# Inverse norms by plain tensor-tensor operations and the feed-forward affine step on ScalarE, in a Mamba and local-attention kernel

## The reference

```python
for i in range(6):
    x = attn_layer(shift_tokens(x), Wqkv[i], q_scale[i], k_scale[i], Wo[i]) + x
    x = ffn_layer(shift_tokens(x), ln_g[i], ln_b[i], W1[i], b1[i], W2[i], b2[i]) + x

def attn_layer(x, Wqkv, qs, ksc, Wo):      # 16 heads of 64, windows of 32 tokens
    q, k, v = jnp.split(x @ Wqkv, 3, -1)
    ...
    q = l2norm(q) * qs                     # t / max(norm(t), 1e-12), per head
    k = l2norm(k) * ksc
    q = q * cos * scale + rotate_half(q) * sin * scale
    k = k * cos / scale + rotate_half(k) * sin / scale
    return local_attention(q, k, v) @ Wo   # softmax over this and the last window

def ffn_layer(x, g, bln, W1, b1, W2, b2):
    xn = (x - mean(x)) / jnp.sqrt(var(x) + 1e-05) * g + bln
    a, gate = jnp.split(xn @ W1 + b1, 2, -1)
    return a * jax.nn.gelu(gate, approximate=False) @ W2 + b2
```

## Time and profile before

| what | us |
|---|---|
| median of 3 runs | 4404.91 (4402.44 to 4407.99) |
| the profiled execution, its own time | 4399.7 |
| its span, first to last instruction | 4397.9 |
| PE, DVE, ACT, POOL busy in the span | 3910.8, 3821.2, 2986.0, 2854.8 |

### The profile page before, as it was taken

One profiled execution on the slowest core, in us unless ns is written; L12 is line 12 of the kernel. 1 busy time (PEld: TensorE's weight loads), 2 busy tenths in 40 slices (PEclk: granted clock), 3 DMA queues, 4 the chain that ended last, 5 costly groups with the idle time before them and its releaser, 6 DMA issues.

```text
span 4397.9 us, 109994 instructions
## 1 busy us (share of the span) xinstructions
PE 3910.8 (89%) x43616; PEld 2578.9 (59%) x43616; DVE 3821.2 (87%) x4101; ACT 2986.0 (68%) x6909; POOL 2854.8 (65%) x1550
## 2 busy tenths in 40 slices
PE   5888888888848999899999999999998999999998
PEld 2333333333326776677767677767776776676675
DVE  3888888888949999899998999889998999989996
ACT  4655564556337777677777777777777777777775
POOL 0555555555637777777777777867777777767773
PEclk8898898898869999999999999999999999999999
DMA  1000000000010000000000000000000000000001
GB/s 39 0 0 0 0 0 0 1 0 1 0 51 5 2 24 2 5 2 14 12 2 5 2 14 12 2 5 2 24 2 5 2 14 12 2 5 2 2 2 40
DMA packets 11922, 34.92 MB, mean 8 GB/s; under 512 B 2382, under 2 KB 4240, under 8 KB 10392
## 3 DMA queue, kind: packets, MB, share of 16 engines
q1 hardware_dynamic: 11416, 27.88, 1.8%
HBM read 23.68 MB, written 4.19 MB: 6 GB/s over the span
## 4 chain that ended last, share of the span: by engine, by line
PE 41%; DVE 12%; issue 9%; ACT 7%; POOL 2%; DMA 0%; DVEq 0%; SPq 0%; ACTq 0%; POOLq 0%
PE ps L771 8%; PE ps L829 6%; PE ps L817 6%; PE ps L782 5%; PE ps L840 4%; DVE sq L1077 4%; DVE resid L1090 3%; PE ps L865 3%; ACT prob L968 3%; PE ps L878 3%; DVE ssq L1042 2%; PE ps L802 2%; ACT L1011 1%; PE ps L853 1%; PE ps L847 1%
## 5 line engine op out<-in xcount | busy, mean ns | idle before, releaser
L425 POOL TENSOR_TENSOR read<-state,c_row 128x1024 f32<-128x1024 f32 x256 | 598.3, 2356 | 620.1 <-DVE state L411 501.4
L1227 POOL TENSOR_TENSOR resid<-resid,sq 128x1024 f32<-128x1024 f32 x384 | 911.7, 2385 | 127.8 <-DVE sq L1077 80.2
L1237 POOL TENSOR_TENSOR resid<-resid,rnorm 128x1024 f32<-128x1024 f32 x384 | 728.9, 1904 | 304.8 <-DVE rnorm L1062 304.8
L771 PE MATMUL ps<-w_qk,xs_parts 128*128 128x512 f32 x2304 | 646.6, 416 | 89.7 <-DVE resid L1090 46.5
L840 PE MATMUL ps<-mixed,w_vo 128*128 128x128 f32 x6144 | 718.7, 275 | 0.1
L840 PEld LDWEIGHTS ps<-mixed,w_vo 128*128 128x128 f32 x6144 | 706.1, 192 | 5.0 <-issue 0.5
L968 ACT ACTIVATE prob<-ps,stat 128x64 f32<-128x64 f32 x3072 | 650.3, 375 | 1.6
L930 ACT ACTIVATE sq<-ps 128x1024 f32<-128x1024 f32 x384 | 410.0, 1068 | 314.1 <-PE ps L771 313.5
L229 PE MATMUL mamba_ps<-read,ident 128*128 128x512 f32 x1024 | 571.9, 697 | 22.4 <-DVE xc L366 19.8
L1090 DVE TENSOR_TENSOR resid<-ps,rope_l 128x1024 f32<-128x1024 f32 x384 | 466.8, 1216 | 116.9 <-ACT sq L930 114.4
L771 PEld LDWEIGHTS ps<-w_qk,xs_parts 128*128 128x128 f32 x2304 | 412.8, 193 | 248.7 <-issue 170.1
(11 more groups left out here) (134 smaller groups left out, 6426.7 us busy)
## 6 DMA issues: line engine op xcount, KB each, us to landing
w_stage<-w_qk_hbm SPq DMA_DIRECT2D x6, 1024.0 KB, 4.9
vo_stage<-w_v_hbm SPq DMA_DIRECT2D x6, 512.0 KB, 3.9
vo_stage<-w_o_hbm SPq DMA_DIRECT2D x6, 512.0 KB, 5.1
xn<-x_hbm SPq DMA_DIRECT2D x4, 512.0 KB, 5.4
kept<-resid SPq DMA_DIRECT2D x8, 256.0 KB, 3.3
resid<-kept SPq DMA_DIRECT2D x8, 256.0 KB, 4.4
out_hbm<-resid SPq DMA_DIRECT2D x8, 256.0 KB, 2.0
w_stage<-w_hbm SPq DMA_DIRECT2D x6, 341.0 KB, 3.2
```

The costliest lines, as they stand in the source:

```text
L425: pool.tensor_tensor(read[:, u % 4, :], state[:, u % 4, :], c_row[:, (u // 2) % 2, :], ALU.mult).then_inc(read_ready, 1)
L771: last = pe.matmul(ps[:, A + c, :], xs_parts[:, odd, xpart, :], w_qk[:, wpart, cols], start=k == 0, stop=k == 2)
L1227: pool.tensor_tensor(qk[:, tile % 2, cols], qk[:, tile % 2, cols], sq[:, 2 + part, :], ALU.add).then_inc(done[f"rotated{part}"], 1)
L1237: pool.tensor_tensor(heads, heads, norms, ALU.mult).then_inc(done[f"normed{part}"], 1)
```

## The change

The guard becomes one tensor-tensor maximum with a column that holds the floor, and no longer halves. The Newton step uses 1.5 - s r r with the s that isn't halved, in four tensor-tensor operations. So that this fits, r is now the inverse root of 2s: the exponential's constant is half a power of two smaller, and the host's rope tables carry a factor of the root of 2. The affine step of the feed-forward norm moves from DVE to ACT, as an activation Identity with a scale and a bias per partition. All four order tables are new. `LAST_GELU`, the index of the gelu behind which the table set is preloaded, is 1 where it was 2. The places for the final additions of the last chunk are shared out anew.

The diff, with the tables cut to the entries that matter:

```diff
--- before
+++ after
 PE_ORDER = [
-    (4, None, "value0"), (2, 2, "score"), (2, 3, "head_turn0"), (2, 3, "head_turn1"), (3, None, "mean"), (2, 0, "mix"),
...
+    (2, 1, "row_turn"), (1, 0, "project1"), (3, 3, "output"), (2, 3, "head_turn0"), (2, 3, "head_turn3"),
...
 ACT_ORDER = [
...
+    (1, 1, "copy_heads3"), (1, 1, "copy_heads0"), (1, 3, "square0"), (3, None, "gelu2"), (1, 2, "inverse_norm"),
...
+    (0, 1, "square1"), (2, None, "log"), (1, 2, "copy_rows"), (2, None, "rstd"), (0, 0, "copy_heads1"),
+    (2, None, "affine"), (0, 3, "round"), (2, None, "round_high"), (1, 1, "copy_mixed0"), (1, 1, "copy_mixed1"),
+    (1, 1, "copy_mixed3"), (1, 1, "copy_mixed2"), (0, 2, "square0"), (0, 1, "inverse_norm"), (1, 3, "exponent"),
+    (0, 0, "copy_heads0"), (2, None, "gelu0"), (1, 3, "copy_rows"), (2, None, "gelu1")]
...
-LAST_GELU = 2
+LAST_GELU = 1
 LOAD_W1_AT, LOAD_QK_AT, LOAD_VO_AT = 2, 20, 16
...
     (wqk_loaded, wvo_loaded, w1_loaded, w2_loaded, scale_loaded, const_loaded, const_set, vo_folded, vo_copied, rope_ready,
      wqk_high, wqk_low, rs_log, newton_step, out_low, w1_high, w1_low, resid_loaded,
      final_low, final_high, stored) = [z[n] for n in names]
-    CONSTS_SET = 4
+    CONSTS_SET = 5
     KEPT = 16 * CHUNKS
 
     def after(eng, *producers):
...
                 after(act, ("guard", tile))
                 if tile >= 2:
                     after(act, ("normed0", tile - 2), ("normed1", tile - 2))
-                act.activation(rnorm[:, odd, :], ssq[:, odd, :], ACT.Ln, scale=float(2 ** (NORM_SHIFT + 1))).then_inc(rs_log, 1)
+                act.activation(rnorm[:, odd, :], ssq[:, odd, :], ACT.Ln, scale=float(2 ** NORM_SHIFT)).then_inc(rs_log, 1)
                 act.wait_ge(rs_log, tile + 1)
                 act.activation(rnorm[:, odd, :], rnorm[:, odd, :], ACT.Exp, scale=-0.5,
                                bias=exp_shift[:, 0:1]).then_inc(done["inverse_norm"], 1)
...
             def rstd(chunk):
                 after(act, ("log", chunk))
                 act.activation(work[:, :], work[:, :], ACT.Exp, scale=-0.5).then_inc(done["rstd"], 1)
+
+            def affine(chunk):
+                l = chunk // CHUNKS
+                if chunk % CHUNKS == 0:
+                    act.wait_ge(w2_loaded, 32 * l + 32)
+                after(act, ("scale", chunk))
+                act.activation(xc[:, :], xc[:, :], ACT.Identity, scale=lp[:, l % 2, LN_G:LN_G + 1],
+                               bias=lp[:, l % 2, LN_B:LN_B + 1]).then_inc(done["affine"], 1)
 
             def round_chunk(chunk):
                 after(act, ("affine", chunk))
...
         def _(dve):
             dve.memset(ones_mean[:, :], 1.0 / DIM).then_inc(const_set, 1)
             dve.memset(eps_col[:, :], EPS).then_inc(const_set, 1)
-            dve.memset(one_half[:, :], 0.5).then_inc(const_set, 1)
-            dve.memset(exp_shift[:, :], float(np.log(2.0) * NORM_SHIFT / 2)).then_inc(const_set, 1)
+            dve.memset(norm_floor[:, :], NORM_FLOOR).then_inc(const_set, 1)
+            dve.memset(three_halves[:, :], 1.5).then_inc(const_set, 1)
+            dve.memset(exp_shift[:, :], float(np.log(2.0) * (NORM_SHIFT - 1) / 2)).then_inc(const_set, 1)
             dve.wait_ge(const_set, CONSTS_SET)
 
             def table(part, i, tile):
...
             def guard(tile):
                 after(dve, ("squares0", tile), ("squares1", tile))
                 s = ssq[:, tile % 2, :]
-                dve.scalar_tensor_tensor(out=s, in0=s, scalar=NORM_FLOOR, in1=one_half[:, 0:1].to_broadcast([P, 2 * HEADS]),
-                                         op0=ALU.max, op1=ALU.mult).then_inc(done["guard"], 1)
+                dve.tensor_tensor(s, s, norm_floor[:, 0:1].to_broadcast([P, 2 * HEADS]), ALU.max).then_inc(done["guard"], 1)
 
             def refine(tile):
 
                 after(dve, ("inverse_norm", tile))
                 r, step = rnorm[:, tile % 2, :], newton[:, :]
-                dve.scalar_tensor_tensor(out=step, in0=ssq[:, tile % 2, :], scalar=-1.0, in1=r,
-                                         op0=ALU.mult, op1=ALU.mult).then_inc(newton_step, 1)
-                dve.wait_ge(newton_step, 2 * tile + 1)
+                dve.tensor_tensor(step, ssq[:, tile % 2, :], r, ALU.mult).then_inc(newton_step, 1)
+                dve.wait_ge(newton_step, 3 * tile + 1)
                 dve.tensor_tensor(step, step, r, ALU.mult).then_inc(newton_step, 1)
-                dve.wait_ge(newton_step, 2 * tile + 2)
-                dve.scalar_tensor_tensor(out=r, in0=step, scalar=1.5, in1=r, op0=ALU.add, op1=ALU.mult
-                                         ).then_inc(done["refine"], 1)
+                dve.wait_ge(newton_step, 3 * tile + 2)
+                dve.tensor_tensor(step, three_halves[:, 0:1].to_broadcast([P, 2 * HEADS]), step, ALU.subtract).then_inc(newton_step, 1)
+                dve.wait_ge(newton_step, 3 * tile + 3)
+                dve.tensor_tensor(r, r, step, ALU.mult).then_inc(done["refine"], 1)
 
             def table_ready(part, tile):
                 l, t, odd = place(tile)
...
                 dve.tensor_tensor(xc[:, :], shifted(xb, chunk % CHUNKS * BANK, BANK), turn_bank("mean", chunk),
                                   ALU.subtract).then_inc(done["centre"], 1)
 
-            def affine(chunk):
-                l = chunk // CHUNKS
-                if chunk % CHUNKS == 0:
-                    dve.wait_ge(w2_loaded, 32 * l + 32)
-                after(dve, ("scale", chunk))
-                dve.tensor_scalar(xc[:, :], xc[:, :], lp[:, l % 2, LN_G:LN_G + 1], lp[:, l % 2, LN_B:LN_B + 1], ALU.mult,
-                                  ALU.add).then_inc(done["affine"], 1)
-
             def product(k):
                 m = HIDDEN_PARTS[k][1]
 
...
     angle = np.arange(SEQ)[:, None] * (10000.0 ** (-half / HEAD_DIM))[None]
     power = (np.arange(SEQ) - SEQ // 2) / (WINDOW // 2)
     scale = ((half + 0.4 * HEAD_DIM) / (1.4 * HEAD_DIM))[None] ** power[:, None]
-    cos, sin = np.cos(angle), np.sin(angle)
+
+    cos, sin = np.sqrt(2.0) * np.cos(angle), np.sqrt(2.0) * np.sin(angle)
     tables = [np.concatenate(v, axis=1) for v in ((QK_SCALE * cos * scale,) * 2, (-QK_SCALE * sin * scale, QK_SCALE * sin * scale),
                                                   (cos / scale,) * 2, (-sin / scale, sin / scale))]
     t = np.stack(tables).astype(np.float32).reshape(4, SEQ_TILES, P, HEAD_DIM)
```

More of the change, by code:

```diff
@@ L521 @@
-LAST_GELU = 2
+    (2, 1, "row_turn"), (1, 0, "project1"), (3, 3, "output"), (2, 3, "head_turn0"), (2, 3, "head_turn3"),
+    (1, 1, "project0"), (4, None, "value2"), (2, 2, "score"), (2, 3, "head_turn2"), (2, 3, "head_turn1"),
+    (3, None, "mean"), (2, 0, "mix"), (1, 1, "project1"), (3, None, "variance"), (2, 2, "row_turn"), (4, None, "value1"),
+    (1, 0, "head_turn1"), (2, 3, "score"), (2, 1, "mix"), (1, 2, "project0"), (4, None, "ff_output"),
[5 rows of a table added]
+    (2, 2, "output")]
+ACT_ORDER = [
[6 rows of a table added]
+    (1, 1, "exponent"), (0, 2, "round"), (1, 1, "copy_rows"), (1, 3, "copy_heads0"), (1, 3, "copy_heads3"),
+    (0, 1, "square0"), (0, 0, "inverse_norm"), (1, 3, "copy_heads2"), (1, 3, "copy_heads1"), (1, 2, "exponent"),
+    (2, None, "square"), (1, 0, "copy_mixed0"), (1, 0, "copy_mixed2"), (1, 0, "copy_mixed1"), (1, 0, "copy_mixed3"),
+    (0, 1, "square1"), (2, None, "log"), (1, 2, "copy_rows"), (2, None, "rstd"), (0, 0, "copy_heads1"),
+    (2, None, "affine"), (0, 3, "round"), (2, None, "round_high"), (1, 1, "copy_mixed0"), (1, 1, "copy_mixed1"),
+    (1, 1, "copy_mixed3"), (1, 1, "copy_mixed2"), (0, 2, "square0"), (0, 1, "inverse_norm"), (1, 3, "exponent"),
+    (0, 0, "copy_heads0"), (2, None, "gelu0"), (1, 3, "copy_rows"), (2, None, "gelu1")]
@@ L569, in engine_sequences @@
     last = ALL_CHUNKS - 1
-    spare = sorted(dve.index((name, last)) for name in ("centre", "affine", "product0", "product1", "product2"))
-    finals = [[dve[spare[0]], 0, 1], [dve[spare[1]], 2, 3]] + [[dve[i], 4 + k] for k, i in enumerate(spare[2:])] + [[("add_ff", last), 7]]
+    spare = sorted(dve.index((name, last)) for name in ("centre", "product0", "product1", "product2"))
+    finals = [[dve[spare[0]], 0, 1, 2], [dve[spare[1]], 3], [dve[spare[2]], 4], [dve[spare[3]], 5, 6], [("add_ff", last), 7]]
     for place, *chunks in finals:
@@ L611, in transformer @@
     eps_col = sb("eps_col2", [P, 1])
-    one_half = sb("one_half", [P, 1])
+    norm_floor = sb("norm_floor", [P, 1])
+    three_halves = sb("three_halves", [P, 1])
     exp_shift = sb("exp_shift", [P, 1])
@@ L1020, in _ @@
                       **indexed("copy_mixed", copy_mixed, WINDOWS),
-                      "square": square_chunk, "log": log, "rstd": rstd, "round_high": round_chunk, **indexed("gelu", gelu, 3)}
+                      "square": square_chunk, "log": log, "rstd": rstd, "affine": affine, "round_high": round_chunk, **indexed("gelu", gelu, 3)}
             for name, k in ACT_SEQ:
@@ L1175, in _ @@
```

(2 more changed lines are left out.)

26 lines of the change are left out of this document (8 added, 18 removed), and 37 rows, old and new, of tables (ACT_ORDER, DVE_ORDER, PE_ORDER, POOL_ORDER).

## The result

The changed kernel took 4762.28 us (median of 4 runs, 4756.89 to 4768.58), the kernel before 4403.67 (4401.17 to 4407.99) beside it. The ratio is 1.0814, with a 95% interval of 1.0795 to 1.0832: 8% slower, 359 us. The prediction was slower, 4610 us in a range of 4500 to 4790.

What follows compares the result with a forecast made beforehand. PE bounded the kernel at 61.70 us a period; ACT would then, at 62.5 + 2.2 + 1.1 = 65.8. Adding 193 us and 10 for the last chunk to 4399.7 gave 4603, with offset 4610; range 4540 to 4700, wider 4500 to 4790.

Steps and rivals of the forecast that it cites:

- The cause: On ACT, the preload behind gelu1 is undone by gelu2: 602 table loads against 96, 506 more, 1.31 us each.
- ACT's work per period: Per transformer chunk, ACT's busy time: 47.53 + 14.4 for loads + 0.63 for the affine step = 62.5 us.
- The waits of ACT: Per period, ACT waits 2.2 us at the squares and 1.1 us for POOL's scale, making the pace 65.8 us.
- the bank pair: Two shared banks for projections, read by ACT's square and DVE's rope products before PE projects again: ACT waits 2.2 us.
- the lower bound: Whole kernel with ACT at 62.5 us a period and never waiting: 4453 us; the upper bound was 5068.
- The signs: Expected profile: 602 loads, ACT above 95% busy, period near 66 us, PE near 58.9, DVE near 56.4, guard far above 235 ns.
- Guard and Newton step: On DVE, the plain guard stays held up by POOL, saving 0; the fourth Newton operation adds 0.9 us a period.
- This slack buys nothing: DVE falls from 57.97 to 56.4 us a period, but ACT becomes the limit, so no time is gained.
- Rival 1: ACT is full but its waits vanish as PE runs ahead: 4453 us, spread to 4530; chance 0.14.
- Rival 2: Late inverse norms delay POOL, PE's head turns and ACT's copies: pace 70 us, 4807 us in all; chance 0.18.
- Rival 3: Logarithm and exponential share a table set, PE keeps the pace at 59.5 us a period: 4302 us; chance 0.03.
- 8 loads: The number of loads per period up to which ACT would stay under PE's 58.9 us, making the kernel faster.

Runs made afterwards that it cites:

- the repaired kernel: The changed kernel with only the table-set preload put back behind gelu2 (LAST_GELU 2): 4325.33 us, ratio 0.9816 to the kernel before.
- the last experiments: Changed kernel with LAST_GELU 2 plus two 128x1280 ACT copies a chunk: ahead of the second projection's square 4323.11 us, behind gelu1 4449.55 us.

## Why the prediction was right, and where it was off

**The cause** was right. The surplus loads are the 506 that were counted in the built order, 1283 ns each. Taking them away alone gives the whole loss back and more, in the new order (437 us) and with the sign turned in the old (404 us). In the trace of the front norms a logarithm and an exponential had a load each, and that held for the inverse norms too.

**ACT's work per period** was right: forecast 62.5, measured 62.84 us. The affine step was set at 0.63 by a cast and took 0.82 us. With loads at 1.31 us the rest fits.

**The waits of ACT** were the step that failed in size. The forecast had 3.3 us a period at "two places", 2.2 around the squares and 1.1 for the scale. Here are all of ACT's waits of 0.3 us or more in the period of 70.00 us (start, us, what; idle before and for whom in brackets):

```profile
2269.11 0.82 ACT L1002 ACTIVATE xc_ff<-xc_ff,lp 128x512 f32<-128x512 f32 x1 [0.90 <-POOL xc_ff L1250]
...
2271.82 2.06 ACT L979 COPY mixed<-ps 128x512 f32<-128x512 f32 x4 [1.18 <-PE ps L831]
...
2289.19 2.06 ACT L979 COPY mixed<-ps 128x512 f32<-128x512 f32 x4 [1.27 <-PE ps L831]
...
2291.90 0.38 ACT L961 COPY rows<-ps 128x256 f32<-128x256 f32 x1 [0.46 <-PE ps L795]
...
2294.16 1.03 ACT L932 ACTIVATE sq<-ps 128x1024 f32<-128x1024 f32 x1 [0.42 <-PE ps L773]
...
2307.31 1.07 ACT L954 COPY q_t<-ps 128x512 f32<-128x512 f32 x2 [0.32 <-PE ps L784]
2309.57 1.03 ACT L932 ACTIVATE sq<-ps 128x1024 f32<-128x1024 f32 x1 [1.19 <-PE ps L773]
...
2315.87 1.02 ACT L932 ACTIVATE sq<-ps 128x1024 f32<-128x1024 f32 x1 [0.95 <-PE ps L773]
```

They add up to 6.69 us, and with the shorter ones ACT's idle time is 70.00 - 62.84 = 7.16 us, where the sum had 3.3. This term is what was mis-sized: 3.9 us a period, 181 us over 47 periods. The scale's wait is the first, 0.90 us. The stretch with the bank pair is the last three, 0.32 + 1.19 + 0.95 = 2.46 us, where 2.2 had been worked out. So both places that were counted were right in size. What was left out are the other four, 3.33 us, above all the two waits for `mix`, 1.18 and 1.27. How the second comes about is seen best in another period. ACT first, then PE:

```profile
2579.05 0.70 ACT L1021 ACTIVATE hidden<-ps,lp 128x512 f32<-128x512 f32 x1
2579.78 1.28 ACT L1024 ACT_TABLE_LOAD   x1
2581.07 1.07 ACT L954 COPY k_t<-ps 128x512 f32<-128x512 f32 x2
2582.03 1.04 ACT L932 ACTIVATE sq<-ps 128x1024 f32<-128x1024 f32 x1
2584.34 2.06 ACT L979 COPY mixed<-ps 128x512 f32<-128x512 f32 x4 [1.27 <-PE ps L831]
```

```profile
2579.87 1.64 PE L773 MATMUL ps<-w_qk,xs_parts 128*128 128x512 f32 x6
2582.29 2.00 PE L831 MATMUL ps<-prob_t,rows 32*128 32x512 f32 x16 [0.78 <-ACT k_t L954]
```

The preload at 2579.78 stands ahead of the two copies of k. PE's next `mix` takes all four turning banks, and two of them are still to be read by these copies. So PE starts 0.78 us late, at 2582.29, right behind the copies; and ACT, after its square, waits 1.27 us for this same `mix`. A load on ACT first makes PE late and then comes back to ACT as a wait.

The wait of 1.18 us begins in the same way, with a `mix` that had to wait for ACT, here for the copy of q behind the loads of `log` and `rstd`. But TensorE's clock has its part in it. PE's `mix`, then the stretch of its first half and a whole period with a faster one (columns as in the earlier trace rows):

```profile
2268.35 3.40 PE L831 MATMUL ps<-prob_t,rows 32*128 32x512 f32 x16 [2.61 <-ACT q_t L954]
```

```profile
2268.30:2270.00 1.70, 1.65 (x8) 0.93 (x12) 1.60 (x3) 0.89 (x2) 1.70 (x2) 0.50 0.00 0
1543.90:1612.60 68.70, 59.22 (x860) 44.34 (x860) 53.68 (x75) 62.72 (x142) 45.35 (x27) 1.00 0.06 21
```

After 2.61 us without work PE ran this `mix` at a granted clock of 0.50, 1.2 GHz in place of 2.4, and it took 3.40 us where others take 2.00. With 2.00 us it would have ended at 2270.35, before ACT was through with `round_high` at 2270.64, and ACT would not have waited. Of the 47 `mix` at this place 31 took over 2.2 us, and ACT waited 30.7 us for them in all. The fall of the clock does not follow every such wait: in the period from 1543.90 the `mix` took 2.00 us behind a wait of 2.59, the granted clock was 1.00, and the period was 68.7 us long. So of the 4.2 us by which the pace was off, about 1.3 are the clock's in the period of 70.00 us, and 0.7 on average (30.7 / 47).

In its period of 59.50 us the repaired kernel has five of these eight waits at the same length (0.91 us for the scale, then 0.48, 0.42, 0.32 and 1.21), and the one for the `mix` behind gelu1 at 0.94. What the loads filled are others: 3.66 us ahead of the last square became 0.95, and 1.74 for a head turn and 0.60 ahead of the square behind gelu1 went. The wait for the scale and the one of 1.21 us at the bank pair are round trips, in which another engine starts only when ACT has done its part, and ACT has nothing else to do in between; they did not get shorter when ACT got more to do elsewhere.

The forecast had followed the shared pair of banks as the one loop between ACT and PE. It had not followed the four turning ones, and had no term for PE's clock. It named ACT's 14.2 us of idle time as a reason to stay near the lower bound; that is the reasoning that fell. The two copies in the last experiments show it plainly: the same 2.6 us of work cost nothing at one place and 124 us at another.

**The total.** The 47 periods with the changes of layer were forecast at 3153 us and took 3330.15, 177 more. The longer pace gives 4.2 x 47 = 197, and what lies over 47 x 70.00 was 40 us and not 60. With the 177 us the forecast of 4610 becomes 4787, 25 more than measured. Of these, 10 are the loads of the last chunk: outside the 47 periods the changed kernel took 1436.65 us and the kernel before 1437.66, so that term did not show. Another 11 are that the profiled execution was taken as 5.2 us below the median, and here was 6.3 above it. The forecast's own range, 4540 to 4700, was too narrow upward; the wide one holds the time.

**The signs.** 602 loads of 1283 ns and a guard far above 235 ns came as named. ACT was to be busy for over 95% of a period and was for 90%, the period was to be near 66 us and was 70, and PE was busy for 60.63 us in it, not 58.9, of which the slow `mix` is 1.4.

**Guard and Newton step.** Right: no gain from the plain form, alone it is 27 us dearer. That POOL holds up the plain form as well bore out in the run with these edits alone, 777 ns for the plain guard against 729.

**Affine step and DVE's slack.** "This slack buys nothing" was right for the changed kernel, where DVE fell to 53.82 us (56.4 forecast; the guard takes 652 ns where it took 729, and no Newton operation over 252). In the old order the move alone cost 18 us, which nothing in the prediction had priced.

**The rivals.** Rival 1 (ACT full, no waits) was wrong: ACT still waited 7.16 us a period. Rival 2 gave the size, a pace of 70 us, and a part of its mechanism is in the trace:

```profile
PE ps L831 <- DVE xb L1135: 85.5, 47, 2.7
```

PE's `mix` waits 85.5 us in all for DVE's `add_output` (0.8 in the repaired kernel). At 2301.93 us it waits 1.71 us, and DVE comes late there because its Newton step had waited 2.82 us for the inverse norm. But in that period ACT waits for a head turn only 0.32 us, as in the repaired kernel, so this lateness did not come back to ACT as rival 2 had it; that its pace fits is in part luck. Rival 3, faster, was wrong as it was put, for the set was not shared. Its price for a kernel with few loads, 59.5 us a period and 4302 us, came out in the repaired kernel, at 59.50 us and 4325. Its reason, that a freed DVE lets PE go, is not shown: the affine step alone cost 18 us in the old order, and which part of the new order gives the gain was not tried. (Its "8 loads" are loads added to the two, so 10 a period, against 13 in the built order.)

## What to carry to other kernels

A table load, or any filler, costs what the engine that waits behind it loses, and an engine's idle time is slack only at the place in its order where it lies; ask of each added instruction which buffers the next ones will free, and who takes those. Where an order of work is rewritten, look again at everything that is attached to a position in it, here a preload behind "the last" of three stages, and read the built instructions, not the source.

## What was not expected of the hardware

The loads themselves did nothing unexpected: with copies of the same length at their places the time was 4722 against 4762 us. Unexpected was how far place matters: 11 copies of 1.29 us a chunk cost 397 us at one set of places and 648 us at another, while two of 1.25 us cost nothing at one place and 124 us at another. The granted TensorE clock is a second cost of making PE wait. Its mean of 0.98 in the period of 70.00 us looks harmless, but the half speed fell on the `mix` behind PE's longest wait, and ACT paid for it with 1.18 us. Over the 47 periods the same 40047 matmuls kept PE busy for 2772.85 us at 0.99 in the kernel before and for 2855.54 us at 0.97 in the changed one.
